# A deformable-convolution block on one core: the test for far sampling points moves from VectorE to ScalarE and TensorE, and four subtractions become one

## What is computed

```python
x1 = silu(bn(depthwise_conv3x3(x)))                  # "conv's taps": nine matmuls
offset = x1 @ off_w + off_b                          # 8 groups x 9 points x (x, y)
mask = softmax((x1 @ mask_w + mask_b).reshape(N, H, W, 8, 9), -1)
...
samples = _bilinear_sample(img, sg)                  # at the position + tap + offset
out = (samples * m).sum(-1)
```

## Time and profile before

| | |
|---|---|
| median of 3 runs | 707.15 us (706.99 to 709.14) |
| the profiled execution | 709.08 us, span 707.3 us |
| DVE busy | 580.2 us, 82% of the span |
| PE busy | 585.4 us, 83% |
| ACT busy | 227.5 us, 32% |
| POOL busy | 316.1 us, 45% |
| mean granted TensorE clock | 0.932 of full speed |

### The profile page before, as it was taken

How to read it: one execution, slowest core, us unless ns; L and a number is a source line. 1 busy time by engine, 2 the same in 40 slices (tenths; PEclk the granted TensorE clock), 3 DMA queues, 4 the chain that set the end, 5 groups by cost and what they waited for, 6 DMA issues and landing times.

```text
span 707.3 us, 11117 instructions
## 1 busy us (share of the span) xinstructions
PE 585.4 (83%) x3456; PEld 432.8 (61%) x3456; DVE 580.2 (82%) x1052; ACT 227.5 (32%) x334; POOL 316.1 (45%) x326
## 2 busy tenths in 40 slices
PE   5992877888868869978888679889999999929995
PEld 3462655666546557556566567567777777715774
DVE  4579899999999999999999999836777766652766
ACT  6050600612413315206116000234454544413431
POOL 6523795797817796068278240201222211215111
PEclk8786998989999998999989799999999999977998
DMA  7057602003003006000000000000000000004011
GB/s 186 30 186 276 202 0 85 23 2 105 2 1 105 1 3 259 1 1 3 0 1 3 0 1 1 1 0 1 1 1 1 1 1 1 1 15 105 30 46 44
DMA packets 25594, 30.54 MB, mean 43 GB/s; under 512 B 5188, under 2 KB 17684, under 8 KB 25556
## 3 DMA queue, kind: packets, MB, share of 16 engines
q1 hardware_dynamic: 24654, 29.77, 12.8%
q0 software_dynamic: 896, 0.23, 0.4%
q10 hardware_dynamic: 6, 0.00, 0.0%
HBM read 24.94 MB, written 5.05 MB: 42 GB/s over the span
## 4 chain that ended last, share of the span: by engine, by line
PE 47%; DVE 25%; issue 13%; DVEq 2%; ACT 1%; POOL 0%; POOLq 0%; ACTq 0%
DVE prod L1391 11%; PE banks L797 10%; PE banks L912 8%; PE pair L892 8%; DVE stencil L1367 5%; DVE outer L1361 5%; PE pair L968 4%; PE banks L902 4%; PE banks L1002 4%; PE pair L750 3%; PE pair L743 2%; DVEq L1391 1%; PE banks L884 1%; PE banks L819 1%; PE banks L863 1%
## 5 line engine op out<-in xcount | busy, mean ns | idle before, releaser
L797 PE MATMUL banks<-ident,prod 128*128 128x128 f32 x1568 | 226.2, 291 | 79.5 <-DVE prod L1391 77.3
L797 PEld LDWEIGHTS banks<-ident,prod 128*128 128x128 f32 x1568 | 186.8, 149 | 139.5 <-DVE prod L1391 115.6
L1391 DVE TENSOR_TENSOR prod<-shifted,stencil 128x1024 f32 (+1 forms) x224 | 238.1, 1086 | 6.2 <-PE banks L797 6.2
L1187 POOL TENSOR_TENSOR rstd_now<-mv_now,neg_half 128x2 f32<-128x2 f32 x32 | 23.0, 718 | 131.6 <-DVE mv_now L1443 131.6
L750 PE MATMUL pair<-xg,dw_diag 128*128 128x512 f32 x144 | 73.9, 615 | 1.2 <-ACT dw_diag L514 1.2
L1159 POOL CAST far_list_i<-far_list 1x8 int32<-1x8 f32 x8 | 33.9, 4237 | 85.2 <-DVE far_list L1377 57.2
L912 PE MATMUL banks<-shifted 128*128 128x128 f32 x512 | 63.3, 277 | 2.3 <-ACT shifted L651 1.4
L912 PEld LDWEIGHTS banks<-shifted 128*128 128x128 f32 x512 | 60.2, 192 | 8.1 <-issue 6.1
L1361 DVE TENSOR_TENSOR outer<-hats 128x800 f32<-128x800 f32 x64 | 63.1, 987 | 0.8
L1367 DVE TENSOR_TENSOR stencil<-stencil,outer 128x800 f32 (+1 forms) x64 | 62.9, 983 | 0.3
L892 PE MATMUL pair<-shifted 128*128 128x512 f32 x128 | 61.0, 599 | 0.6 <-ACT shifted L634 0.6
(11 more groups left out here) (230 smaller groups left out, 849.0 us busy)
## 6 DMA issues: line engine op xcount, KB each, us to landing
shifted<-padded SPq DMA_DIRECT2D x42, 256.0 KB, 4.0
shifted<-padded SPq DMA_DIRECT2D x14, 640.0 KB, 7.8
res<-in_x_dram SPq DMA_DIRECT2D x4, 512.0 KB, 5.9
padded<-stage SPq DMA_DIRECT2D x4, 512.0 KB, 2.6
stage<-in_L_ffn_W_dram SPq DMA_DIRECT2D x16, 128.0 KB, 2.1
out_dram<-res SPq DMA_DIRECT2D x8, 256.0 KB, 2.3
padded<-stencil SPq DMA_DIRECT2D x2, 228.0 KB, 2.5
got<-padded,cell_now POOLq DMA_INDIRECT x28, 2.8
```

The costliest lines, as they stand in the source:

```text
L797: mm = pe.matmul(acc_of(c, r), prod[:, d % PROD, r * G:(r + 1) * G, :].rearrange("p g c -> p (g c)"), ident[:, :], is_transpose=True, star ...
L1391: ins = ve.tensor_tensor(prod[:, dx:dx + n, :, :], shifted[:, dx:dx + n, bass.ds(((c % HALF) * ROWS + dy) * G, ROWS * G), :], stencil_of[: ...
```

## The change

ACT no longer squares the offsets ahead of the hats. Behind the Relu it runs two Sign passes straight from PSUM, Sign(offset - 2) and Sign(-offset - 2), and writes them in bf16 (`signs`). DVE's maximum and comparison are gone. PE counts with four matmuls of one column against 8192 in place of the one against ones, and the code's constant makes up for the negative signs; a far coordinate counts 2 x 8192. The count stands ahead of tap 27 where it stood ahead of tap 18, and the conv's taps stand ahead of taps 18 to 26 where they stood ahead of 22 to 30. The mask's maximum is subtracted for all four rows in one operation. Of the units, seven instead of five are issued ahead of the maximum, the two that stood in the far test are gone from there, one stands behind the subtraction, and one fewer behind the stencil's last addition.

```diff
-AT_FAR, AT_CONV, AT_SAMPLES, AT_PROJECT = 18, 22, 35, 39
+AT_CONV, AT_FAR, AT_SAMPLES, AT_PROJECT = 18, 27, 35, 39
...
-STENCIL_FILL = (0, 1, 1, 0, 1, 1, 0, 1, 1)
+STENCIL_FILL = (0, 1, 1, 0, 1, 1, 0, 1, 0)
...
-                sc.activation(far_xy, raw[:, :, 0:2 * GP], ACT.Square).then_inc(square_done, 1)
...
+                if not isinstance(k, int) or k > 0:
+                    sc.wait_ge(far_mm, k)
+                    sc.sem_inc(act_waited, 1)
+                for i, sign in enumerate((1.0, -1.0)):
+                    last = sc.activation(signs[:, i, :, :], raw[:, :, 0:2 * GP], ACT.Sign,
+                                         bias=tap_bias[:, TAPS - 1:TAPS], scale=sign)
+                last.then_inc(signs_done, 1)
...
-                    pe.wait_ge(square_done, k)
+                    pe.wait_ge(signs_done, k)
...
-                pe.wait_ge(masks_done, k + 1)
+                pe.wait_ge(signs_done, k + 1)
...
-                count = pair[1][:, 0:FAR_COLS]
-                pe.matmul(count, ones16[:, :], far[:, :], start=True, stop=False)
-                pe.matmul(count, ones[0:1, :], far_codes[:, :], start=False, stop=True).then_inc(far_mm, 1)
+                count = pair[1][0:1, 0:FAR_COLS]
+                pe.matmul(count, ones[0:1, 0:1], far_codes[:, :], start=True, stop=False)
+                for i in range(4):
+                    mm = pe.matmul(count, far_unit[:, :], signs[:, i // 2, :, (i % 2) * GP:(i % 2 + 1) * GP],
+                                   start=False, stop=(i == 3))
+                mm.then_inc(far_mm, 1)
...
-                for r in range(ROWS):
-                    last = ve.tensor_tensor(mask[:, r * G:(r + 1) * G, :], lg[:, r],
-                                            row_max[:, r * G:(r + 1) * G].unsqueeze(2).to_broadcast([P, G, PTS]),
-                                            ALU.subtract)
-                last.then_inc(logits_done, 1)
-
-                ve.wait_ge(square_done, k + 1)
-                own(ve.tensor_tensor(off_most[:, :].rearrange("p (r g) -> p r g", r=ROWS), far_xy[:, :, 0:GP],
-                                     far_xy[:, :, GP:], ALU.max))
+                ve.tensor_tensor(mask[:, :, :].rearrange("p (r g) q -> p r g q", r=ROWS), lg,
+                                 row_max[:, :].rearrange("p (r g) -> p r g", r=ROWS).unsqueeze(3)
+                                 .to_broadcast([P, ROWS, G, PTS]), ALU.subtract).then_inc(logits_done, 1)
                 fill(1)
-                own.wait()
-                own(ve.tensor_scalar(far_flags, off_most[:, :], float(REACH) ** 2, FAR_UNIT, ALU.is_gt, ALU.mult))
-                fill(1)
-                own.wait()
...
                 finish_silu(k + 1)
-                fill(5)
+                fill(7)
                 mask_logits(k + 1, fill)
                 fill(1)
                 masks(k + 1, fill)
```

More of the change, by code:

```diff
@@ L86 @@
 FAR_UNIT = 8192.0
+MOST_CODE = int(FAR_UNIT) * (4 * P + 1) - 1
 PAIRS = B * H // ROWS // 2
@@ L159, in hybrid_block_kernel @@
         bias_all = sb("bias_all", [P, 3, C])
-        bias_parts = sb("bias_parts", [1, 3, 3 * GP + C], BF16)
         bias_parts3 = sb("bias_parts3", [3, 3 * GP + C], BF16)
@@ L184, in hybrid_block_kernel @@
         off_of = off[:, :, :, :].rearrange("p s r o -> p s (r o)")
-        off_most = sb("off_most", [P, ROWS * GP])
-        far = sb("far", [P, FAR_COLS], BF16)
-        far_flags = far[:, :]
+        signs = sb("signs", [P, 2, ROWS, 2 * GP], BF16)
+        bias_parts = signs[0:1, :, :, :].rearrange("p s r o -> p (s r o)")[:, 0:3 * (3 * GP + C)] \
+            .rearrange("p (i o) -> p i o", i=3)
+        far_unit = sb("far_unit", [P, 1], BF16)
         row_max = sb("row_max", [P, ROWS * G])
@@ L193, in hybrid_block_kernel @@
         outer = sb("outer", [P, ROWS * G, TAPS, TAPS])
-        far_xy = outer[:, :, :, :].rearrange("p g a b -> p (g a b)")[:, 0:ROWS * 2 * GP] \
-            .rearrange("p (r o) -> p r o", r=ROWS)
         stencil = sb("stencil", [P, 2, ROWS * G * STENCIL])
@@ L316, in hybrid_block_kernel @@
         bias_in = sem("bias_in")
-        square_done = sem("square_done")
+        signs_done = sem("signs_done")
         stencil_clear = sem("stencil_clear")
@@ L331, in hybrid_block_kernel @@
         hats_done = sem("hats_done")
-        masks_done = sem("masks_done")
         far_mm = sem("far_mm")
@@ L831, in turn @@
                 offsets(k + 1)
-                add_up(k, first_of(BEGIN), AT_FAR)
-                for i in range(AT_FAR, STENCIL):
+                add_up(k, first_of(BEGIN), AT_CONV)
+                for i in range(AT_CONV, STENCIL):
                     if i == AT_FAR:
@@ L1024, in _ @@
             own(gp.memset(ones16[:, :], 1.0))
+            own(gp.memset(far_unit[:, :], FAR_UNIT))
             own(gp.memset(group_mean[:, :], 1.0 / GN_C))
@@ L1051, in _ @@
                 gp.iota(far_codes[:, r * GP:(r + 1) * GP].rearrange("p (g q) -> p g q", g=G),
-                        pattern=[[GROUP_UNIT + PTS, G], [1, PTS]], base=r * G * GROUP_UNIT, **whole)
+                        pattern=[[GROUP_UNIT + PTS, G], [1, PTS]], base=int(FAR_UNIT) * 4 * P + r * G * GROUP_UNIT, **whole)
             gp.iota(corner[:, :].rearrange("p (a b) -> p a b", a=2), pattern=[[B * HP * G, 2], [G, 2]], base=0, **whole)
@@ L1164, in _ @@
                 gp.sem_inc(list_taken, 1)
-                more = gp.value_load(far_list_i[0:1, LIST - 1:LIST], min_val=0, max_val=int(FAR_UNIT) * (P + 1) - 1)
+                more = gp.value_load(far_list_i[0:1, LIST - 1:LIST], min_val=0, max_val=MOST_CODE)
                 with gp.If(more > int(FAR_UNIT) - 1):
@@ L1170, in _ @@
                                                   .rearrange("a s o -> a (s o)"), min_val=0,
-                                                  max_val=int(FAR_UNIT) * (P + 1) - 1)
+                                                  max_val=MOST_CODE)
                             with gp.If(count > int(FAR_UNIT) - 1):
@@ L1177, in _ @@
                     with gp.Fori(0, LIST - 1) as j:
-                        code = gp.value_load(far_list_i[0:1, bass.ds(j, 1)], min_val=0, max_val=int(FAR_UNIT) * (P + 1) - 1)
+                        code = gp.value_load(far_list_i[0:1, bass.ds(j, 1)], min_val=0, max_val=MOST_CODE)
                         with gp.If(code > int(FAR_UNIT) - 1):
@@ L1315, in masks @@
                 own.wait()
-                ve.sem_inc(masks_done, 1)
                 own.link(ve.reciprocal(row_sum[:, :], row_sum[:, :]))
```

## The result

The changed kernel took 726.17 us, median of 4 runs (719.79 to 728.22), against 707.2 before (4 runs, 706.99 to 709.14): 1.0235 times the time, 95% interval 1.0189 to 1.028. Two later sets of the same kernel gave 720.55 (6 runs, 717.55 to 728.67; 1.0157, 1.0121 to 1.0193) and a single 727.89. Beside these later sets the kernel before had medians of 709.07 and 709.12, so times of different sets are best compared by their ratios. The changed kernel is slower by some 11 to 19 us, with a spread of 11 us (717.55 to 728.67) that the kernel before, at 706.2 to 711.6 in all its runs, does not have. The run of 728.67 counts as a slow one and is left out of its set's ratio. The forecast was 713.8, range 705.5 to 718.0.

A forecast was written before the change was run, and what follows sets the result against it. The prediction took DVE's issued work plus its waits to bound each turn. Seven turns at 0.96 us added 6.7, taking the profiled 709.08 to 715.8; that execution being 1.9 above the median, it forecast 713.8, range 705.5 to 718.0.

The forecast's parts named there:

- What bounds the kernel: In the seven turns, what DVE issues plus what it must wait for is a turn's length; DVE 49.24 of 50.68 us busy.
- Work taken from DVE: Per turn, subtractions, far maximum and comparison (1.16 us) go, one subtraction (0.49) comes: DVE's own work falls by 0.67.
- Units moved: Two units now ahead of the maximum make the subtraction later; DVE then waits 1.62 us per turn for ACT's hats.
- What I cost at nothing: Two Sign passes on ACT, PE's larger count and the moved conv taps, all taken to add no time to a turn.
- Net per turn: Weighing starts 2.10 us later with one more unit (1.14) already done, so a turn grows by 0.96 us.
- slower still: Count and taps moved earlier leave PE at its lower clock at turn starts: 2.9 or 9.2 us more; chance 0.13.
- The faster rival: DVE's wait for the hats does not come, only its saved work counts: 4.7 us less, 702.4; chance 0.16.

The follow-up runs named there:

- fill5_tail: Changed kernel with five units ahead of the maximum, three behind the subtraction, and the unit behind the stencil's last addition kept: 704.43 us, ratio 0.9939.
- after_tail: Changed kernel with the unit behind the stencil's last addition kept, taken from behind the first addition: median 718.25 us, ratio 1.0141.
- conv22: Changed kernel with conv taps back ahead of tap 22 and the count behind them, ahead of tap 31: 720.27 us, ratio 1.0149.
- before_conv18: Kernel before with only PE's order as in the change, conv taps ahead of tap 18, count ahead of 27: 707.66 us, ratio 0.9995.
- after_third: The changed kernel, unchanged, run and profiled once more: 727.89 us.
- after_busy: Changed kernel with 16 more transposes, their result unused, on PE at the end of each turn: 717.18 us, ratio 1.0123.
- after: The changed kernel itself, in its first profile: 719.79 us; median of its first set 726.17 us.
- fill5_busy: Changed kernel with five units ahead of the maximum, three behind the subtraction, and 16 unused transposes on PE at each turn's end: 706.75 us, ratio 0.9969.
- before: The kernel without the change: median 707.2 us.

## Why the prediction was wrong, point by point

- **What bounds the kernel**: right. What VectorE issues and what it waits for gives the length of a turn, in every kernel of the table.
- **Work taken from DVE**, 0.67 per turn: right. The one subtraction lasts 0.45 and takes 0.37 of the turn (282.95 to 283.32), where 0.49 was put; fill5_tail gets 5.2 back where 4.7 was worked out.
- **Units moved**: right. The wait for the Relu was forecast at 1.62 in each of seven turns, and is 1.52 in the turn shown and 11.7 in seven. Exp's idle ahead was forecast at about two and is 2.32. With the work saved and nothing else, this costs 6.2 (after_tail; forecast 6.7).
- **What I cost at nothing**: the Sign passes took 1.35 for two where I took the square's 0.65 each, and cost nothing; conv taps and count cost nothing (conv22, before_conv18). The empty place behind the stencil's last addition is not in that list at all, so it too was put at nothing.
- **Net per turn**: this is the step that failed. It gave 0.96 per turn; the stretch of the first profile grew by 10.0, which is 1.43 per turn, and that of after_third by 2.29. "With one more unit (1.14) already done, which is missing behind the stencil's last addition" counted what that unit brings, and not what it covered. The place hid two things. VectorE's next unit needs that addition to be done: with nothing between, it stands up to 0.44, 2.9 in seven turns. And TensorE had the unit's products to add meanwhile: without them it idles 1.9 instead of 0.48 at the turn's end, and then starts the next turn at the lower clock in some turns of some executions.
- **The rival "slower still"** had the effect right and the cause wrong. It put the lower clock down to the moved count and taps; it was TensorE's idle time at the end of the turn. (Of the two only the taps come earlier, as the rival says; the count went from tap 18 to tap 27.) Its prices were 2.9 and 9.2 in all; measured against after_busy's stretch, the clock costs 1.2, 5.5 and 7.2 in the three profiles of the changed kernel.
- **The faster rival**: the work that went to ScalarE and the grouped subtraction do gain, 0.6% in fill5_tail. The condition that the prediction set for it, a subtraction early enough, was not met by this change. The Trainium skill, "Perfetto Trace Analysis", section "Optimizing Scalar/DVE Operations", says that grouping, and giving ScalarE some work of a saturated DVE, can pay; fill5_tail agrees, the changed kernel does not.

The changed kernel's first profile thus adds up, over the stretch: 6.2 for the subtraction's late start less the work saved (after_tail), 2.6 for the empty place (after_busy less after_tail; the own wait alone is 2.9), 1.2 for the clock (411.50 less 410.35), together 10.0. As these are differences between neighbours in one row of kernels, they must add up; what supports the names is that each is near what the waits of its kernel give (1.2 for the clock is also 6.9 less 5.7 of waiting for PE).

Why the first set's median of 726.17 lies 6 above that of the second is not settled: it has three of four executions near 724 to 728, the second one of six. The profile of 727.89 shows where such an execution spends it (5.7 us in the wait for PE, and 2.0 in a first weighing that starts at 45.95 instead of 43.91), but not why it does so in that execution.

## What to carry to other kernels

An instruction moved away is an edit at two places: price the place that it leaves as carefully as the one to which it goes, by asking what ran under its cover on its own engine and on the engine that eats its output. Where work is taken from a saturated engine, keep the producer of another engine's long chain at its old place first, and spend the saved time behind it; here the same saving came out at 4.0 us less (704.43 against 708.44 beside it) or 11.5 more (720.55 against 709.07), by the place of three units. And where TensorE idles just ahead of dense matmuls, look at the granted clock of several executions, since one profile can show the cheapest of them.

## What the runs showed of the hardware that was not expected

- TensorE idle for 1.9 us at a turn's end was followed by the lower clock in some turns and not in others, with the same instructions: 16 matmuls in 2.23 or 3.39 (after, after_third). At the first turn's end the same was seen with 1.05 of idle time (3.67 in after_third, 2.23 in after). With at most 0.17 of idle time it never was: 1.91 to 2.23 at all six turn starts of fill5_busy and of after_busy. What decides between the two stays open. The Trainium skill, "TensorE: Matmul & The Clock Gate", section "Part 1: The HAM clock gate (the "warmup" mystery)", says that the clock is set by how busy the array has been lately, and that the number of slow matmuls in one kernel differs from run to run; these two traces agree.
- Sixteen transposes whose result nobody uses, 1.91 us of TensorE per turn, made the kernel 5.4 us faster (712.2 to 706.75).
- At the emptied place VectorE stood 0.42 to 0.44 us between its addition and the unit that needs it (0.24 in the first turn); with one unit of 1.14 between, it stood not at all. This is not the price of every such pair: in the prologue of before, an addition starts 0.04 behind the end of the product that it reads (49.08 + 0.99 to 50.11). What makes the wait longer at this place stays open.
- A Sign pass over 128x576 from PSUM into bf16 took 724 ns in the mean (16 of them), a little more than the square's 0.65 on the same elements.
